# Masks of the first two weight pairs spread out of a compact block by shuffles, loads on two queues, and the first group's products cut into four batches

## The chip, the cores and the metric

The kernel runs on one core of one Trainium2 chip. The metric is the device time of one execution in microseconds (us); the kernel before takes 66.61 us (median of 3 runs, 66.33 to 66.75). Engines are named as in the profile: PE (TensorE, with its weight loads PEld), DVE (VectorE), ACT (ScalarE), POOL (GpSimd), and SP, whose queue issues most DMAs.

## The reference

```python
# B, N, T, O, G = 32, 256, 256, 256, 8; everything is f32
masked_w = weight * mask[None, :, :]              # (G, O, T)
w_bot = einsum('bg,got->bot', y, masked_w)        # y is cond_8, (B, G)
x = x + einsum('bnt,bot->bno', x, w_bot) + bias   # x is (B, N, T)
```

## The kernel before

The work has two stages. The **small stage** makes the 32 matrices `w_raw[b]` = w_bot[b] + identity (the identity carries the residual). The **large stage** multiplies the 32 batches of x by them, in 8 groups of 4 batches (`NB`), each group in two halves of the outputs, h = 0 and 1.

*Small stage.* The 256 output rows are made in 8 **units** of 32 rows (`UNITS`), two to a **pair** j. PE makes a unit u in `weigh_unit(u)` with 16 products of weight blocks with `y` (`weigh`; 32 matmul instructions in the trace, since f32 takes two passes), in four row groups of the array side by side. A unit has two sides, each a slot of 1024 columns in PSUM (`slots` 0 to 3): on the **diagonal** side PE first lays the identity down (`identity`, two bf16 matmuls), and the mask must already be in the weights, so some engine multiplies these weights by the mask before, in two halves (`masked_by_dve`, `masked_by_pool`). On the **other** side the mask is applied when the unit leaves PSUM. ACT copies the diagonal side to `w_raw` (`raw_by_act`; for unit 1 the sides are swapped), DVE multiplies the other side by its mask into `w_raw` (`raw_by_dve`). The ACT count is n+1 when unit n has left, for n of 2 or more, and so is DVE's. The first two units are made together, `weigh_first_pair`: all products of the other sides, then all of the diagonal sides. A unit may start when the slots that it writes have been emptied:

```python
            if u < SIDES:
                return slots[:, 2 * u + side, :]
            if u < EARLY:
                return slots[:, ((0, 3), (1, 2))[u % 2][side], :]

            return slots[:, ((0, 1), (3, 2))[u % 2][side], :]
```

with `EARLY = 6`. The diagonal side is 1 for even units and 0 for odd ones, so that the diagonal sides of units 2 to 7 are in slots 3, 1, 3, 1, 1, 3.

*Loads.* The data of the small stage lie in one HBM tensor `first` in the order of `ORDER`. A "masked" load of 512 KB has the diagonal weights of a pair and, beside them, their masks (each mask row 8 times, once for each g); it lands in `x_ring`, which later holds x, and the masked weights are written from there to `weights`. An "other" load (256 KB) has the weights of the other sides. All these loads are issued by SP one after the other; ACT issues the small inputs (`smalls`: y, bias and the masks of the first two other sides). DVE masks pairs 0 and 3, POOL pairs 1 and 2 and, in four pieces behind these (`raw_masked`), the side of unit 1 that ACT copied unmasked.

*Large stage.* Group 0 is multiplied in plain f32 straight from `w_raw` (`multiply_first`; a batch of one half is 2 products, 4 matmul instructions in the trace). Of its half 0, batches 0 and 1 stand on PE between units 5 and 6, in a slot of their own (`early`), the other two behind unit 7, and then half 1. Groups 1 to 7 are multiplied as three products of rounded high and low parts: for each group ACT makes `x_hi` and `w_hi`, DVE `x_lo` and `w_lo`, and PE runs 48 matmuls (`multiply_group`, 336 in all). Group 1's `w_hi` and `w_lo` are made in three pieces (`high_piece`, `low_piece`). The orders on all engines are written out by hand.

## Time and profile before

| | |
|---|---|
| median of 3 runs | 66.61 us |
| span of the profiled execution | 65.5 us |
| the profiled execution's own time | not given apart from the span; the median lies 1.1 us above the span |
| PE matmul busy | 58.8 us, 90% |
| DVE, ACT busy | 48.1 and 47.9 us, 73% each |
| POOL busy | 7.0 us, 11% |
| read and written in HBM | 11.73 and 8.39 MB |

Groups of instructions are named by line, engine, operation and tiles (out<-in). "Idle before <-X" is the time in which the engine did nothing just before, and what ended it. A queue's row such as SPq is the issue of a DMA, and its landing is given apart.

### The profile page before, as it was taken

The numbers are of one execution on the slowest core, as the hardware profiler recorded it, in microseconds if no ns is written. First come the engines' busy times: TensorE is split into PE (matmuls) and PEld (weight loads), VectorE is DVE, ScalarE is ACT, GpSimd is POOL, SyncE is SP. The second block draws the span as 40 slices with busy tenths as digits, with TensorE's granted clock in tenths as the row PEclk, the third lists the DMA queues.
The fourth block names the chain that finished last, engine by engine and source line by source line (L and its number), as shares of the span: only waits on it lengthen the run. The fifth ranks groups of instructions, "written<-read, shape, count | busy, mean of one in ns | idle before, by whom it ended". The sixth has DMA issues, their size and how long they took to land.

```text
span 65.5 us, 1501 instructions
## 1 busy us (share of the span) xinstructions
PE 58.8 (90%) x645; PEld 54.3 (83%) x645; DVE 48.1 (73%) x36; ACT 47.9 (73%) x40; POOL 7.0 (11%) x17
## 2 busy tenths in 40 slices
PE   2997188999999999999999999999999999999910
PEld 1266087977888899999999999999999999999900
DVE  2109809999957989999999999989999992250200
ACT  2506609799889999999999799999869986005520
POOL 5500299900000000000000000000000000000000
PEclk9999999999999999999999999999999999999999
DMA  0999999999998157954999999999999229918393
GB/s 0 260 373 306 352 412 422 407 434 428 420 410 340 60 85 255 408 215 198 245 285 225 400 451 420 403 441 423 398 413 425 93 100 408 398 63 325 158 372 116
DMA packets 5334, 20.21 MB, mean 309 GB/s; under 512 B 592, under 2 KB 1104, under 8 KB 4432
## 3 DMA queue, kind: packets, MB, share of 16 engines
q1 hardware_dynamic: 5040, 19.89, 79.6%
q10 hardware_dynamic: 288, 0.23, 1.1%
q8 instruction: 5, 0.08, 0.5%
q14 instruction: 1, 0.01, 0.1%
HBM read 11.73 MB, written 8.39 MB: 307 GB/s over the span
## 4 chain that ended last, share of the span: by engine, by line
PE 79%; DMA 9%; ACT 4%; SPq 2%; issue 1%
PE slots L433 20%; PE slots L431 20%; PE slots L432 20%; PE slots L451 11%; DMA weights<-in_first 9%; PE slots L332 6%; ACT w_raw L534 3%; PE slots L326 2%; ACT weights L563 1%; SPq L230 1%; SPq L222 1%; SPq L229 1%
## 5 line engine op out<-in xcount | busy, mean ns | idle before, releaser
L431 PE MATMUL slots<-x_hi,w_hi 128*128 128x256 f32 x112 | 31.4, 280 | 0.0
L432 PE MATMUL slots<-x_lo,w_hi 128*128 128x256 f32 x112 | 31.2, 279 | 0.0
L433 PE MATMUL slots<-x_hi,w_lo 128*128 128x256 f32 x112 | 31.2, 279 | 0.0
L431 PEld LDWEIGHTS slots<-x_hi,w_hi 128*128 128x128 f32 x112 | 21.1, 188 | 0.0
L432 PEld LDWEIGHTS slots<-x_lo,w_hi 128*128 128x128 f32 x112 | 21.1, 188 | 0.0
L433 PEld LDWEIGHTS slots<-x_hi,w_lo 128*128 128x128 f32 x112 | 21.1, 188 | 0.0
L589 DVE TENSOR_TENSOR x_lo<-x_ring,x_hi 128x2048 fp32r<-128x2048 f32 (+1 forms) x8 | 16.1, 2022 | 0.5 <-ACT x_hi L491 0.5
L491 ACT CAST x_hi<-x_ring 128x2048 fp32r<-128x2048 f32 (+1 forms) x8 | 13.5, 1694 | 1.3 <-DMA x_ring<-in_x 1.3
L511 ACT ACTIVATE weights<-slots,smalls 128x1024 f32<-128x1024 f32 x10 | 10.8, 1112 | 4.7 <-PE slots L433 4.7
L598 DVE TENSOR_TENSOR w_lo<-w_raw,w_hi 128x2048 fp32r<-128x2048 f32 x6 | 13.7, 2288 | 0.2 <-ACT w_hi L499 0.2
L499 ACT CAST w_hi<-w_raw 128x2048 fp32r<-128x2048 f32 x6 | 11.5, 1909 | 0.0
L332 PE MATMUL slots<-smalls,weights 32*128 32x128 f32 x256 | 9.3, 279 | 2.0 <-DMA weights<-in_first 1.6
L332 PEld LDWEIGHTS slots<-smalls,weights 32*128 32x128 f32 x256 | 8.2, 186 | 3.0 <-DVE w_raw L631 1.9
L534 ACT COPY w_raw<-slots 128x1024 f32<-128x1024 f32 x7 | 7.0, 1014 | 3.8 <-PE slots L332 3.7
L635 DVE TENSOR_TENSOR w_raw<-slots,masks_off 128x1024 f32<-128x1024 f32 x6 | 7.1, 1220 | 2.0 <-PE slots L332 1.8
L451 PE MATMUL slots<-x_ring,w_raw 128*128 128x256 f32 x32 | 7.4, 386 | 0.2
L451 PEld LDWEIGHTS slots<-x_ring,w_raw 128*128 128x128 f32 x32 | 5.9, 190 | 1.3 <-ACT w_raw L534 0.5
L615 DVE TENSOR_SCALAR weights<-slots,smalls 128x1024 f32<-128x1024 f32 x4 | 5.1, 1282 | 2.4 <-PE slots L433 2.4
L581 DVE TENSOR_TENSOR weights<-x_ring 128x256 f32<-128x256 f32 x4 | 1.5, 420 | 3.1 <-DMA x_ring<-in_first 3.1
L306 POOL TENSOR_TENSOR weights<-x_ring 128x256 f32<-128x256 f32 x4 | 2.8, 727 | 5.2 <-ACT w_raw L534 5.0
L440 PE MATMUL slots<-zeros 128*128 128x512 bf16 x5 | 2.3, 626 | 1.2 <-DVE zeros L571 1.2
L605 DVE TENSOR_TENSOR w_lo<-w_raw,w_hi 128x512 fp32r<-128x512 f32 (+1 forms) x3 | 2.5, 866 | 1.2 <-ACT w_hi L502 1.2
(25 smaller groups left out, 19.3 us busy)
## 6 DMA issues: line engine op xcount, KB each, us to landing
out<-weights SPq DMA_DIRECT2D x15, 512.0 KB, 4.7
x_ring<-in_x SPq DMA_DIRECT2D x7, 1024.0 KB, 9.6
x_ring<-in_first SPq DMA_DIRECT2D x6, 512.0 KB, 7.2
weights<-in_first SPq DMA_DIRECT2D x4, 256.0 KB, 6.6
out<-weights SPq DMA_DIRECT2D x1, 256.0 KB, 2.4
out<-weights SPq DMA_DIRECT2D x1, 128.0 KB, 2.3
out<-weights ACTq DMA_DIRECT2D x1, 128.0 KB, 2.1
smalls<-in_small ACTq DMA_DIRECT2D x1, 97.0 KB, 3.1
```

The source lines that it names most:

```text
L332: return nc.tensor.matmul(bank(u, i)[:, q * B * RT:(q + 1) * B * RT], weights_of(u, i // PER)[rows, q * P:(q + 1) * P], y[rows], start=not ...
L431: nc.tensor.matmul(dst, wh, xh, start=(k == 0), stop=False)
L432: nc.tensor.matmul(dst, wh, xl, start=False, stop=False)
L433: last = nc.tensor.matmul(dst, wl, xh, start=False, stop=(k == KC - 1))
L451: last = nc.tensor.matmul(dst[:, (b - lo) * N:(b - lo + 1) * N], w_raw[:, b, k * O + h * P:k * O + (h + 1) * P], x_ring[:, 0, first_x(k, b ...
L491: nc.scalar.copy(part_x(x_hi[:, g % RS], lo, hi), part_x(x_ring[:, g % XS], lo, hi)).then_inc(x_hi_ready, 1)
L499: nc.scalar.copy(part(w_hi, g), raw_part(g)).then_inc(w_hi_ready, 1)
L511: nc.scalar.activation(result(g, h), product(g, h), ACT.Identity, bias=bias(h)).then_inc(done, 1)
L534: nc.scalar.copy(raw_slot(u, True), made(u, True)).then_inc(raw_by_act, 1)
L589: nc.vector.tensor_tensor(part_x(x_lo[:, g % RS], lo, hi), part_x(x_ring[:, g % XS], lo, hi), part_x(x_hi[:, g % RS], lo, hi).bitcast(F32) ...
L598: nc.vector.tensor_tensor(part(w_lo, g), raw_part(g), part(w_hi, g).bitcast(F32), ALU.subtract).then_inc(w_lo_ready, 1)
L635: nc.vector.tensor_tensor(raw_slot(u, False), made(u, False), mask_off_of(u).unsqueeze(2).broadcast_to([P, PER * QU, B, RT]), ALU.mult).th ...
```

## The change

- **Masks.** The diagonal masks of pairs 0 and 1 no longer come eightfold: a compact block of 128x256 values (128 KB) is appended to `smalls`, and DVE spreads it with four `stream_shuffle` instructions of 128x256, each of which copies one row of every eight to all eight, into a quarter of the last place of `x_ring` (`mask_half`). Masks of pairs 2 and 3 still come eightfold, as 256 KB loads to the same place.
- **Loads.** The diagonal weights go straight to `weights`. From pair 1 on, diagonal and other weights of a pair are one load of 512 KB (`pair`). ACT's queue issues, behind `smalls` (97 KB before, 225 KB now), the diagonal weights of pair 0 (256 KB) and the masks of the other sides (96 KB). In all 384 KB less are read.
- **Masking.** POOL masks all four pairs in place, and `mask_raw` of unit 1 is done in one piece behind pair 1 and three behind pair 3. DVE masks none.
- **Order on PE.** `EARLY` is 4: behind each of units 4 to 7 stands one batch of group 0's half 0, in slot 1. Units 5 to 7 start with two products of the other side ahead of the identity. `unit_slot` gives units 5 to 7 the slots (3, 2), (0, 3), (3, 2).
- ACT and DVE make the first two pieces of group 1's weights one unit later or interleaved with the last units, and ACT empties group 0's half 0 in one instruction of 1024 columns, not in two of 512.

The core of the diff:

```diff
-EARLY = 6
+EARLY = 4
 WARM = 5
 
-ORDER = (("other", 0), ("masked", 0), ("masked", 1), ("other", 1), ("off", 0), ("masked", 2), ("other", 2), ("x", 0),
-         ("masked", 3), ("other", 3), ("x", 1))
-COLUMNS = {"masked": SLOT, "other": BANK, "off": (UNITS - SIDES) * SPAN, "x": WIDE // 2}
+ORDER = (("other", 0), ("masked", 0), ("pair", 1), ("off", 0), ("pair", 2), ("mask", 2), ("x", 0),
+         ("pair", 3), ("mask", 3), ("x", 1))
+COLUMNS = {"masked": BANK, "other": BANK, "pair": SLOT, "mask": BANK, "off": (UNITS - SIDES) * SPAN, "x": WIDE // 2}
...
-            if u < EARLY:
+            if u <= EARLY:
                 return slots[:, ((0, 3), (1, 2))[u % 2][side], :]
 
-            return slots[:, ((0, 1), (3, 2))[u % 2][side], :]
-
-
-        early = slots[:, 3, 0:BANK]
+            return slots[:, ((0, 3), (3, 2))[u % 2][side], :]
...
-                sp.dma_start(staged(j), in_order("masked", j)).then_inc(masked_loaded[j], 16)
-                sp.dma_start(blocks[:, 2 * j + 1, :], in_order("other", j)).then_inc(others_loaded[j], 16)
+                sp.dma_start(weights[:, j, :], in_order("pair", j)).then_inc(pair_loaded[j - 1], 16)
+                if j >= SPREAD:
+                    sp.dma_start(mask_rows[:, j * BANK:(j + 1) * BANK], in_order("mask", j)).then_inc(mask_loaded[j - SPREAD], 16)
...
                 return sp.dma_start(x_ring[:, 0, i * SLOT:(i + 1) * SLOT], in_order("x", i))
 
-            sp.dma_start(blocks[:, 1, :], in_order("other", 0)).then_inc(others_loaded[0], 16)
-            sp.dma_start(staged(0), in_order("masked", 0)).then_inc(masked_loaded[0], 16)
+            sp.dma_start(blocks[:, 1, :], in_order("other", 0)).then_inc(first_others_loaded, 16)
             load_pair(1)
-            sp.dma_start(masks_off[:].rearrange("p u m r -> p (u m r)"), in_order("off", 0)).then_inc(masks_off_loaded, 16)
             load_pair(2)
             load_half(0).then_inc(half_x_loaded, 16)
             load_pair(3)
             load_half(1).then_inc(x_loaded[0], 16)
             load_group(1)
-
-
-            sp.wait_ge(masked_by_dve, 2)
-            sp.wait_ge(masked_by_pool, 2)
-            load_group(XS - 2)
-
-            sp.wait_ge(masked_by_pool, 2 * (PAIRS - 2))
-            sp.wait_ge(masked_by_dve, 4)
+            load_group(2)
+
+            sp.wait_ge(masked_by_pool, 2 * PAIRS)
             load_group(XS - 1)
 
             for g in range(GROUPS - 1):
...
-            behind_pair = (None, (0,), (1, 2, 3))
-            for j in range(1, PAIRS - 1):
-
-                pool.wait_ge(masked_loaded[j], 16)
+            def mask_pair(j):
+
+                pool.wait_ge(first_masked_loaded if j == 0 else pair_loaded[j - 1], 16)
+                if j >= SPREAD:
+                    pool.wait_ge(mask_loaded[j - SPREAD], 16)
                 for i in range(2):
-                    nc.gpsimd.tensor_tensor(blocks[:, 2 * j, half_of(i)], staged(j)[:, 0:BANK][:, half_of(i)],
-                                            staged(j)[:, BANK:SLOT][:, half_of(i)], ALU.mult).then_inc(masked_by_pool, 1)
-
-
-                if j == 1:
-                    pool.wait_ge(smalls_loaded, 16)
-                    pool.wait_ge(raw_by_act, 1)
-                for i in behind_pair[j]:
-                    some = raw_columns(1, False)[:, i * MB:(i + 1) * MB, :]
-                    nc.gpsimd.tensor_tensor(some, some, smalls[:, AT_MASKS + SPAN:AT_MASKS + 2 * SPAN].unsqueeze(1).broadcast_to(
-                        [P, MB, SPAN]), ALU.mult).then_inc(raw_masked, 1)
+                    if j < SPREAD:
+                        pool.wait_ge(mask_spread, 2 * j + i + 1)
+                    nc.gpsimd.tensor_tensor(blocks[:, 2 * j, half_of(i)], blocks[:, 2 * j, half_of(i)],
+                                            mask_half(2 * j + i), ALU.mult).then_inc(masked_by_pool, 1)
+
+            def mask_raw(i):
+
+                some = raw_columns(1, False)[:, i * MB:(i + 1) * MB, :]
+                nc.gpsimd.tensor_tensor(some, some, smalls[:, AT_MASKS + SPAN:AT_MASKS + 2 * SPAN].unsqueeze(1).broadcast_to(
+                    [P, MB, SPAN]), ALU.mult).then_inc(raw_masked, 1)
+
+            mask_pair(0)
+            mask_pair(1)
+
+            pool.wait_ge(smalls_loaded, 16)
+            pool.wait_ge(raw_by_act, 1)
+            mask_raw(0)
+            mask_pair(2)
+            mask_pair(3)
+            for i in range(1, B // MB):
+                mask_raw(i)
 
         @block.tensor
         def _(pe):
...
-                if u < EARLY:
-
-                    pe.wait_ge(raw_by_act, u - 1)
-                elif u == EARLY:
-
-                    pe.wait_ge(raw_by_act, u)
-                else:
-
-                    pe.wait_ge(early_by_act, 1)
+                def others_first():
+
+                    pe.wait_ge(raw_by_dve, u - 1)
+                    if u % 2 == 0:
+
+                        pe.wait_ge(pair_loaded[u // 2 - 1], 16)
+                    weigh(u, off, 0)
+                    weigh(u, off + 1, 0)
+
+                if u > EARLY:
+                    others_first()
+
+                pe.wait_ge(raw_by_act, u if u > EARLY else u - 1)
                 identity(u, on)
                 identity(u, on + 1)
-
-                pe.wait_ge(raw_by_dve, u - 1)
-                if u % 2 == 0:
-
-                    pe.wait_ge(others_loaded[u // 2], 16)
-                weigh(u, off, 0)
-                weigh(u, off + 1, 0)
+                if u <= EARLY:
+                    others_first()
                 for q in range(QU):
-                    if u == EARLY and q % 2 == 0:
-
-                        pe.wait_ge(masked_by_dve, 3 + q // 2)
-                    elif u % 2 == 0 and q % 2 == 0:
-
-                        pe.wait_ge(masked_by_pool, u - 1 + q // 2)
+                    if u % 2 == 0 and q % 2 == 0:
+
+                        pe.wait_ge(masked_by_pool, u + 1 + q // 2)
...
             weigh_first_pair()
-            for u in range(SIDES, EARLY):
+            for u in range(SIDES, UNITS):
                 weigh_unit(u)
-
-
-            pe.wait_ge(raw_by_act, EARLY - 1)
-            pe.wait_ge(raw_by_dve, UNITS // HO)
-            pe.wait_ge(raw_masked, 1)
-            pe.wait_ge(half_x_loaded, 16)
-            multiply_first(early, 0, 0, NB // 2).then_inc(early_ready, 1)
-
-            for u in range(EARLY, UNITS):
-                weigh_unit(u)
-
-            pe.wait_ge(raw_by_act, UNITS - 1)
-            pe.wait_ge(x_loaded[0], 16)
-            multiply_first(product(0, 0)[:, BANK:SLOT], 0, NB // 2, NB).then_inc(products_ready, 1)
+                if u >= EARLY:
+                    b = u - EARLY
+                    if b == 0:
+
+                        pe.wait_ge(raw_by_act, UNITS // HO)
+                        pe.wait_ge(raw_by_dve, UNITS // HO)
+                        pe.wait_ge(raw_masked, 1)
+                        pe.wait_ge(half_x_loaded, 16)
+                    if b == NB // 2:
+                        pe.wait_ge(x_loaded[0], 16)
+                    last = multiply_first(product(0, 0)[:, b * N:(b + 1) * N], 0, b, b + 1)
+            last.then_inc(products_ready, 1)
             pe.wait_ge(raw_by_act, UNITS)
             pe.wait_ge(raw_by_dve, UNITS)
             multiply_first(product(0, 1), 1, 0, NB).then_inc(products_ready, 1)
...
             act.dma_start(smalls[:], small).then_inc(smalls_loaded, 16)
+            act.dma_start(blocks[:, 0, :], in_order("masked", 0)).then_inc(first_masked_loaded, 16)
+            act.dma_start(masks_off[:].rearrange("p u m r -> p (u m r)"), in_order("off", 0)).then_inc(masks_off_loaded, 16)
...
-                if u == EARLY:
+                if u == EARLY + 1:
 
                     act.wait_ge(raw_by_act, UNITS // HO)
                     act.wait_ge(raw_by_dve, UNITS // HO)
                     act.wait_ge(raw_masked, 1)
-                    high_piece(0)
-                    high_piece(1)
-
-                    act.wait_ge(smalls_loaded, 16)
-                    act.wait_ge(early_ready, 1)
-                    nc.scalar.activation(result(0, 0)[:, 0:BANK], early, ACT.Identity, bias=bias(0)).then_inc(early_by_act, 1)
+                if u in (EARLY + 1, EARLY + 2):
+                    high_piece(u - EARLY - 1)
 
                 act.wait_ge(diagonal_ready, u + 1)
                 nc.scalar.copy(raw_slot(u, True), made(u, True)).then_inc(raw_by_act, 1)
...
-            mask_pair(0)
+            dve.wait_ge(smalls_loaded, 16)
+            compact = smalls[:, AT_COMPACT:AT_COMPACT + COMPACT]
+            for c in range(CHUNKS):
+                nc.vector.stream_shuffle(mask_half(c), compact, [G * (i // G) + c for i in range(ROWS)]).then_inc(mask_spread, 1)
```

On PE, from behind unit 5 on, before: L451 is a product of group 0, L326 the identity, L332 a product of a unit. The rows are two batches, unit 6, and the identity of unit 7.

```order
L451 MATMUL slots<-x_ring,w_raw 128x256 [waits raw_masked,half_x_loaded,raw_by_dve,raw_by_act]
L451 MATMUL slots<-x_ring,w_raw 128x256 x3
L326 MATMUL slots<-one_of,one_at 128x512 [waits raw_by_act]
L326 MATMUL slots<-one_of,one_at 128x512
L332 MATMUL slots<-smalls,weights 128x128 [waits others_loaded3,raw_by_dve]
L332 MATMUL slots<-smalls,weights 128x128
L332 MATMUL slots<-smalls,weights 128x128 [waits masked_by_dve]
L332 MATMUL slots<-smalls,weights 128x128 x7
L332 MATMUL slots<-smalls,weights 128x128 [waits masked_by_dve]
L332 MATMUL slots<-smalls,weights 128x128 x5
L326 MATMUL slots<-one_of,one_at 128x512 [waits early_by_act]
L326 MATMUL slots<-one_of,one_at 128x512
```

PE now, from behind unit 4 on: L453 is a product of group 0, L332 the identity, L338 a product of a unit. The rows are a batch, unit 5, a batch, and the start of unit 6.

```order
L453 MATMUL slots<-x_ring,w_raw 128x256 [waits raw_masked,half_x_loaded,raw_by_dve,raw_by_act]
L453 MATMUL slots<-x_ring,w_raw 128x256
L338 MATMUL slots<-smalls,weights 128x128 [waits raw_by_dve]
L338 MATMUL slots<-smalls,weights 128x128
L332 MATMUL slots<-one_of,one_at 128x512 [waits raw_by_act]
L332 MATMUL slots<-one_of,one_at 128x512
L338 MATMUL slots<-smalls,weights 128x128 x14
L453 MATMUL slots<-x_ring,w_raw 128x256 x2
L338 MATMUL slots<-smalls,weights 128x128 [waits pair_loaded3,raw_by_dve]
L338 MATMUL slots<-smalls,weights 128x128
L332 MATMUL slots<-one_of,one_at 128x512 [waits raw_by_act]
L332 MATMUL slots<-one_of,one_at 128x512
```

Before, two batches stood in one block behind unit 5; now one batch stands behind each unit, and every identity from unit 5 on waits for ACT's copy of the unit just ahead.

The DMAs that SP issues for the small stage before, in order:

```order
L229 DMA weights<-in_first 128x512
L230 DMA x_ring<-in_first 128x1024
L222 DMA x_ring<-in_first 128x1024
L223 DMA weights<-in_first 128x512
L232 DMA masks_off<-in_first 128x192
L222 DMA x_ring<-in_first 128x1024
L223 DMA weights<-in_first 128x512
L227 DMA x_ring<-in_first 128x1024
L222 DMA x_ring<-in_first 128x1024
L223 DMA weights<-in_first 128x512
L227 DMA x_ring<-in_first 128x1024
```

SP's issues now, up to the second half of group 0's x (the row with x2 is pairs 1 and 2), and behind them the start of ACT's order:

```order
L233 DMA weights<-in_first 128x512
L225 DMA weights<-in_first 128x1024 x2
L227 DMA x_ring<-in_first 128x512
L231 DMA x_ring<-in_first 128x1024
L225 DMA weights<-in_first 128x1024
L227 DMA x_ring<-in_first 128x512
L231 DMA x_ring<-in_first 128x1024
```

```order
L483 DMA smalls<-in_small 128x450
L484 DMA weights<-in_first 128x512
L485 DMA masks_off<-in_first 128x192
L518 ACT_TABLE_LOAD
L518 COPY w_raw<-slots 128x8x32x4 [waits others_ready]
L532 COPY w_raw<-slots 128x8x32x4 [waits diagonal_ready] x4
```

The diagonal weights of pair 0 moved from SP's second place to ACT's queue behind `smalls`, and pair 1, with both its sides, to SP's second place.

On POOL, the masking before:

```order
L306 TENSOR_TENSOR weights<-x_ring 128x256 [waits masked_loaded1]
L306 TENSOR_TENSOR weights<-x_ring 128x256
L315 TENSOR_TENSOR w_raw<-w_raw,smalls 128x8x32 [waits raw_by_act,smalls_loaded]
L306 TENSOR_TENSOR weights<-x_ring 128x256 [waits masked_loaded2]
L306 TENSOR_TENSOR weights<-x_ring 128x256
L315 TENSOR_TENSOR w_raw<-w_raw,smalls 128x8x32 x3
```

and now:

```order
L304 TENSOR_TENSOR weights<-weights,x_ring 128x256 [waits mask_spread,first_masked_loaded]
L304 TENSOR_TENSOR weights<-weights,x_ring 128x256 [waits mask_spread]
L304 TENSOR_TENSOR weights<-weights,x_ring 128x256 [waits mask_spread,pair_loaded1]
L304 TENSOR_TENSOR weights<-weights,x_ring 128x256 [waits mask_spread]
L310 TENSOR_TENSOR w_raw<-w_raw,smalls 128x8x32 [waits raw_by_act,smalls_loaded]
L304 TENSOR_TENSOR weights<-weights,x_ring 128x256 [waits mask_loaded2,pair_loaded2]
L304 TENSOR_TENSOR weights<-weights,x_ring 128x256
L304 TENSOR_TENSOR weights<-weights,x_ring 128x256 [waits mask_loaded3,pair_loaded3]
L304 TENSOR_TENSOR weights<-weights,x_ring 128x256
L310 TENSOR_TENSOR w_raw<-w_raw,smalls 128x8x32 x3
```

Four more instructions stand here, two of them in front of everything else.

## Rows read from the trace of the kernel before

**Rows 1.** Page, chain that ended last: shares of the span by engine.
```profile
PE 79%; DMA 9%; ACT 4%; SPq 2%; issue 1%
```

**Rows 2.** Windows: length, busy time by engine, granted clock, DMA share, GB/s.
```profile
core 0: us, PE busy (x) PEld busy (x) DVE busy (x) ACT busy (x) POOL busy (x), PEclk, DMA share, GB/s
4.00:8.00 4.00, 2.43 (x70) 1.85 (x66) 3.02 (x4) 2.02 (x2) 0.29 (x1) 1.00 0.96 331
8.00:12.00 4.00, 3.35 (x98) 3.20 (x102) 2.21 (x3) 1.97 (x2) 3.80 (x7) 1.00 1.03 414
23.30:62.40 39.10, 39.10 (x336) 38.89 (x334) 32.28 (x18) 32.15 (x24) 0.00 (x0) 1.00 0.81 305
```

**Rows 3.** Loads: issue (start us, us), then KB and us to landing.
```profile
weights<-in_first SPq DMA_DIRECT2D x1, 256.0 KB, 2.9
smalls<-in_small ACTq DMA_DIRECT2D x1, 97.0 KB, 3.1
1.17 0.43 SPq L230 DMA_DIRECT2D x_ring<-in_first  x1
x_ring<-in_first SPq DMA_DIRECT2D x1, 512.0 KB, 3.8
1.65 0.42 SPq L222 DMA_DIRECT2D x_ring<-in_first  x1
x_ring<-in_first SPq DMA_DIRECT2D x1, 512.0 KB, 6.0
```

**Rows 4.** Timeline of PE: start us, us, instructions [idle before, releaser].
```profile
5.46 1.17 PE L332 MATMUL slots<-smalls,weights 32*128 32x128 f32 x32 [0.41 <-DVE weights L581]
8.43 1.34 PE L332 MATMUL slots<-smalls,weights 32*128 32x128 f32 x30 [1.59 <-DMA weights<-in_first]
...
11.00 0.39 PE L326 MATMUL slots<-one_of,one_at 32*128 32x512 bf16 x2 [0.22 <-ACT w_raw L534]
12.08 0.39 PE L326 MATMUL slots<-one_of,one_at 32*128 32x512 bf16 x2
...
13.42 1.99 PE L451 MATMUL slots<-x_ring,w_raw 128*128 128x256 f32 x8
15.35 0.39 PE L326 MATMUL slots<-one_of,one_at 32*128 32x512 bf16 x2
...
17.75 5.45 PE L451 MATMUL slots<-x_ring,w_raw 128*128 128x256 f32 x24
22.84 0.47 PE L431 MATMUL slots<-x_hi,w_hi 128*128 128x256 f32 x1
```

**Rows 5.** Timeline of ACT: units 2, then 4 and 5, then group 0.
```profile
9.93 1.02 ACT L534 COPY w_raw<-slots 128x1024 f32<-128x1024 f32 x1 [2.24 <-PE slots L332]
12.36 2.14 ACT L534 COPY w_raw<-slots 128x1024 f32<-128x1024 f32 x2 [0.46 <-PE slots L332]
25.48 0.68 ACT L545 ACTIVATE weights<-slots,smalls 128x512 f32<-128x512 f32 x1
```

**Rows 6.** Timeline of POOL: the masks of pair 1.
```profile
7.71 1.41 POOL L306 TENSOR_TENSOR weights<-x_ring 128x256 f32<-128x256 f32 x2 [5.05 <-ACT w_raw L534]
```

**Rows 7.** Timeline of DVE: masks of pair 0, units 6 and 7, x_lo of group 2.
```profile
4.99 0.76 DVE L581 TENSOR_TENSOR weights<-x_ring 128x256 f32<-128x256 f32 x2 [3.11 <-DMA x_ring<-in_first]
...
16.56 2.36 DVE L635 TENSOR_TENSOR w_raw<-slots,masks_off 128x1024 f32<-128x1024 f32 x2
...
26.00 2.29 DVE L589 TENSOR_TENSOR x_lo<-x_ring,x_hi 128x2048 fp32r<-128x2048 f32 x1
```

**Rows 8.** Windows, behind the last matmul.
```profile
62.50:65.30 2.80, 0.00 (x0) 0.00 (x0) 0.00 (x0) 0.41 (x1) 0.00 (x0) 1.00 0.66 244
65.38:65.46 0.08, 0.00 (x0) 0.00 (x0) 0.00 (x0) 0.00 (x0) 0.00 (x0) 0.57 0.00 0
```

More of the change, by code:

```diff
@@ L675, with diagonal_of @@
     w_rows, m_rows = rows_of(weight), rows_of(np.broadcast_to(mask, (G, O, T)))
-    diagonal = [np.stack((a[2 * j + 1][0], a[2 * j][0])).reshape(P, BANK) for j in range(PAIRS) for a in (w_rows, m_rows)]
+    def diagonal_of(a, j):
+        return np.stack((a[2 * j + 1][0], a[2 * j][0])).reshape(-1, BANK)
+    mask_in = np.concatenate([diagonal_of(m_rows, j) for j in range(SPREAD)], axis=1)
+    mask_in = np.concatenate([mask_in[r, r % CHUNKS * COMPACT:(r % CHUNKS + 1) * COMPACT] for r in range(P)]).reshape(P, COMPACT)
     loads = {}
     for j in range(PAIRS):
-        loads["masked", j] = np.concatenate(diagonal[2 * j:2 * j + 2], axis=1)
-        loads["other", j] = np.stack((w_rows[2 * j][1], w_rows[2 * j + 1][1]))
+        other = np.stack((w_rows[2 * j][1], w_rows[2 * j + 1][1])).reshape(P, BANK)
+        if j == 0:
+            loads["masked", 0], loads["other", 0] = diagonal_of(w_rows, 0), other
+        else:
+            loads["mask", j] = diagonal_of(m_rows, j)
+            loads["pair", j] = np.concatenate([diagonal_of(w_rows, j), other], axis=1)
     for i in range(2):
```

48 lines of the change are left out of this document (21 added, 27 removed).

## The prediction

> **What bounds the kernel now.** The page comes first: PE holds 79% of the chain that ended last, DMA 9% and ACT 4% [rows 1]. The windows say where the small shares lie: from 23.30 to 62.40 PE is busy without a gap, 336 matmuls in 39.10 us [rows 2], so a group of 48 takes 5.59 us, and nothing in this change touches a matmul of it. What the change can win or lose lies ahead of the first of them, at 22.84 [rows 4], and the matter is when this one starts. The timeline of PE shows the waits there: 1.59 us until 8.43 for the loads of pair 1, 0.22 until 11.00 for ACT's copy of unit 2 [rows 4], and small ones behind. I call 11.00, the start of unit 4's identity, the **hand-over**. From there to group 1 it is 11.84 us.
>
> **Loads.** I write L for the time at which the diagonal weights of pair 0 have landed. Before, they landed with their masks at 1.17 + 3.8 = 4.97, with 865 KB in all issued up to them (256 + 97 + 512). Pair 1's masked load landed at 1.65 + 6.0 = 7.65, at 1377 KB [rows 3]. Between the two stand 512 KB in 2.68 us, 191 KB per us, though the engines move 414 GB/s from 8 to 12 us and 331 from 4 to 8 [rows 2]: a load has landed when its slowest share has.
>
> Now the weights of pair 0 stand behind 225 KB of smalls on ACT's queue, beside SP's queue. Which queue goes ahead is seen in one place: the 256 KB on SP's queue and the 97 KB on ACT's were issued together and landed after 2.9 and 3.1 us [rows 3], so neither waited for all of the other. If the queues take turns row by row, the 256 rows ahead on ACT's queue (128 of smalls, 128 of weights) go beside 256 rows of SP's, 128 of 2 KB and 128 of 4 KB: 225 + 256 + 256 + 512 = 1249 KB, which on the line through the two landings is 4.97 + 384/191 = 6.98. The nearest row of a landing is that at 1377 KB, 7.65. SP's queue ran alone while smalls were still starting, so that more than 1249 KB may be ahead: I take **L = 7.3**, bounds 5.9 (1249 KB with no laggard: 384 KB at 414 GB/s behind 4.97) and 7.65. The Trainium skill ("DMA: Bandwidth & Descriptors", Issuing engines are not separate DMA queues) says that DMAs of different engines run on the same 16 DMA engines and interleave, and that a second issuing engine saves only issue time. The two landings agree. By it, the second queue brings pair 0 nothing, and the sum keeps L = 7.3; without it L could be that of a queue served first, which is a rival below.
>
> **First pair to hand-over.** POOL now masks pairs 0 and 1, four multiplications. Two took 1.41 us together and began 0.06 us behind the landing, at 7.71 [rows 6]; DVE's two took 0.76 [rows 7]. The four end at L + 0.06 + 2.82 = L + 2.88. From the end of pair 1's masks (7.71 + 1.41 = 9.12) to the hand-over it took 11.00 − 9.12 = 1.88 [rows 4, 6]: the rest of unit 2 on PE, ACT's copy of 1.02 from 9.93 [rows 5], and the identity. So the hand-over is at L + 4.76 = 12.06, **1.06 later** than before. PE does not bind there: the first pair's 32 matmuls take 1.17 us [rows 4] and follow the masks half by half. The shuffles are not in the trace. The nearest rows are DVE's multiplications of the same 128x256 values, 0.38 each [rows 7]; even at double that, the four would end at about 4.3 + 3.0 = 7.3, beside the load of the weights, and only the first two are wanted by L + 0.8. I take 0. If the weights landed by 5, that cover would be gone, and the first shuffle would cost up to 0.8. The 384 KB that are no longer read make pairs 2 and 3 and x land earlier; the waits of PE before were not for these, so this is 0. A gain is not excluded where pair 1 lands earlier, but POOL comes to it only at L + 1.5.
>
> **Hand-over to group 1.** Units 4, 5, 6 and 7 all put their diagonal side in slot 3 now, so each identity waits for ACT's copy of the unit ahead. A turn of this ring: identity to copy 12.36 − 11.00 = 1.36 [rows 4, 5], copy 1.01 (half of the 2.14 of two, less the wait between them; the single one is 1.02), and copy to identity 11.00 − 10.95 = 0.05, together 2.42. PE has less to do in a turn: a unit is 12.08 − 11.00 = 1.08, a batch is four of the 24 instructions that ran from 17.75 to 22.84, 0.85 [rows 4]; 1.93 in all, so 0.5 us of each turn PE stands. Three turns take unit 7's identity to hand-over + 7.26. Then half 1 of group 0 waits for both sides of unit 7: DVE's multiplication began 16.56 − 15.35 = 1.21 behind an identity and takes 1.2 (two take 2.36) [rows 4, 7], with 0.05 to PE 2.47. Half 1 is 16 instructions, 3.39. Sum 7.26 + 2.47 + 3.39 = 13.12, against 11.84: **1.28 later**. The wait for DVE's masks of pair 3, ahead of unit 6, and that for `early` are inside the 11.84 and go; late instead is the ring. Bounds: 1.93 a turn if the ring did not bind (4 × 1.93 + 3.39 = 11.1, −0.7), and 2.6 if ACT's first piece of group 1's weights, which now stands between the copies of units 4 and 5, were to touch it; PE's 1.36 hides it.
>
> **Groups 1 to 7.** Before, `x_lo` of group 2 was ready at 28.29 [rows 7], when PE came for it at 22.84 + 5.59 = 28.43, 0.14 to spare. ACT and DVE work off the same list behind unit 7, so that counts from the end of DVE's unit 7, 16.56 + 2.36 = 18.92: ready 9.37 later. PE now comes 0.05 + 3.39 + 5.59 = 9.03 behind it, since only half 1 stands there and not 12 of group 0's 16 products: a wait of 0.34. ACT's finishing of group 0's half 0 goes over 1024 columns instead of 512 (0.68 [rows 5]), which may push `x_hi` of group 4 by some tenths. I take **0.4** for both, bounds 0 and 0.6. Load 3 of x waits for all of POOL's masks, at about L + 7, and is needed far behind.
>
> **The sum.** 1.06 + 1.28 + 0.4 = 2.74 on the span of 65.5, 68.2; the median of 66.61 lies 1.1 above the span, so **69.35**. With L from 6.98 to 7.65 and the groups' bounds it is 68.7 to 69.9.
>
> **Rivals.**
> *The clock falls.* PE's longest wait before, 1.59, left the granted clock at 1.00. Now PE has nothing from some 5.4 (first pair's other sides, a little later than before) until L + 0.8 = 8.1, 2.7 us. Behind the last matmul the clock was 1.00 up to 65.30 and fell inside 65.38 to 65.46 (0.57 is a mean of both levels), 3.0 us behind PE's end [rows 8]; so 2.7 lies near. At 1.2 GHz the units' 1.1 us become 2.2 for some us: the first pair's second half +0.5, unit 2 +0.5, unit 3 +0.5, together 1.5, time 70.85. For: the gap. Against: it is shorter than that at the end, and work stands around it. The Trainium skill ("TensorE: Matmul & The Clock Gate", Part 1) says that the full clock is withdrawn when the array has been idle; by that this rival holds if the idle stretch is long enough.
> *ACT's queue goes first.* Pair 0 then lands with about as much ahead as before, near 5, and pair 1 is last, with all 1249 to 1345 KB ahead, 7.0 to 7.5. POOL masks it at once: hand-over 7.25 + 0.06 + 1.41 + 1.88 = 10.6, 0.4 earlier, sum +1.3, **67.9**.
> *No laggards.* This is the one on the other side. The slow shares between 5 and 7.65 need not come again, and then pairs 0 and 1 both land at about 5.9. In the better order the hand-over is at 5.9 + 3.35 = 9.25, −1.75; the ring still costs 1.28, the groups 0 to 0.4: −0.5 to −0.1, **66.3**. It decides from a hand-over of 9.3 on; to be faster by over 1% it would have to be 8.7, or the ring not bind. Against: there are 2.7 us between two landings 512 KB apart.
> *The change doesn't do what it says.* If the shuffles took over 1 us each, the masks would be late and not the weights; that would look like the forecast, with DVE as releaser, and cost more.
>
> **Numbers.** About 1% of the time, 0.67 us, is what a measurement of this kernel can tell from no change. Forecast 0.55; clock 0.15; ACT's queue first 0.15; no laggards 0.12; the rest 0.03. No laggards gives half of "same" and some of "faster", the second rival a little of "same": faster 0.05, same 0.11, slower 0.84. The range runs from the lower end of the second rival, 67.3, to the clock's price, 70.8; below lie some 0.13, above 0.05.
>
> **What would show it.** The landing of pair 0's diagonal weights between 7.0 and 7.65, and POOL's first mask right behind it; the identity of unit 4 near 12.1; identities of units 5, 6, 7 spaced by 2.42, with ACT's copy as releaser and about 0.5 idle on PE each time; group 1's first matmul near 25.2; a wait of some 0.3 on DVE's `x_lo` at group 2; 39.1 us of matmuls as before. A landing by 6, or units spaced by less than 2.1, would make the forecast wrong; so would a granted clock under 1 between 8 and 14.

## The result: 70.69 us, slower by the ratio 1.0553 (1.0434 to 1.0671)

| | before | after |
|---|---|---|
| median (runs) | 66.47 us (66.24 to 66.75, 4) | 70.69 us (69.66 to 70.79, 4) |
| a profiled execution: time, span | 66.33, 64.5 us (e7, below) | 70.79, 68.7 us |
| read in HBM | 11.73 MB | 11.34 MB |

The ratio rests on the runs within 1.5% of the fastest of each kernel, for the changed one 70.60 and 69.66; the medians stand at 1.0635. Spans of its four runs: 68.7, 68.7, 68.5 and 67.5.

The timeline of PE after the change; the rows answer to [rows 4] (start, length, instructions, idle before and its releaser; L338 is a product of a unit, L332 the identity, L453 a product of group 0, L433 a group's product):

```profile
4.34 1.17 PE L338 MATMUL slots<-smalls,weights 32*128 32x128 f32 x32 [0.30 <-DMA smalls<-in_small]
7.38 1.99 PE L338 MATMUL slots<-smalls,weights 32*128 32x128 f32 x32 [1.86 <-POOL weights L304]
9.12 0.64 PE L332 MATMUL slots<-one_of,one_at 32*128 32x512 bf16 x2
9.15 2.02 PE L338 MATMUL slots<-smalls,weights 32*128 32x128 f32 x30
...
12.40 0.39 PE L332 MATMUL slots<-one_of,one_at 32*128 32x512 bf16 x2 [0.21 <-ACT w_raw L532]
...
14.82 0.39 PE L332 MATMUL slots<-one_of,one_at 32*128 32x512 bf16 x2
...
17.22 0.39 PE L332 MATMUL slots<-one_of,one_at 32*128 32x512 bf16 x2
...
19.62 0.39 PE L332 MATMUL slots<-one_of,one_at 32*128 32x512 bf16 x2
...
22.13 3.69 PE L453 MATMUL slots<-x_ring,w_raw 128*128 128x256 f32 x16 [0.17 <-DVE w_raw L625]
25.57 0.39 PE L433 MATMUL slots<-x_hi,w_hi 128*128 128x256 f32 x1
```

The first row's 32 instructions take 1.17 us, the second's 1.99: the granted clock reads 1.00 from 7.0 to 7.5 and 0.55 from 7.5 to 8.0, so it fell just behind the start of the second row. The hand-over (unit 4's identity) is at 12.40, the four identities from there on stand 2.40 to 2.42 apart, and group 1 starts at 25.57. The windows (length, busy time of PE, PEld, DVE, ACT and POOL, granted clock, DMA share, GB/s) answer to [rows 2] and show the clock and the groups:

```profile
8.00:10.00 2.00, 2.00 (x44) 2.00 (x41) 0.56 (x1) 0.62 (x1) 2.00 (x5) 0.50 1.03 416
10.00:12.00 2.00, 2.00 (x59) 1.99 (x54) 1.47 (x2) 1.06 (x2) 1.48 (x3) 0.76 1.03 399
12.00:14.00 2.00, 1.79 (x44) 1.44 (x37) 1.85 (x3) 1.54 (x3) 2.00 (x4) 1.00 1.06 426
25.57:65.45 39.88, 39.88 (x337) 39.68 (x336) 33.02 (x18) 33.34 (x24) 0.00 (x0) 1.00 0.78 296
```

The DMA issues of the start (KB, us to landing), answering to [rows 3]:

```profile
weights<-in_first SPq DMA_DIRECT2D x1, 512.0 KB, 4.9
weights<-in_first SPq DMA_DIRECT2D x1, 256.0 KB, 3.4
weights<-in_first ACTq DMA_DIRECT2D x1, 256.0 KB, 5.4
smalls<-in_small ACTq DMA_DIRECT2D x1, 225.0 KB, 3.6
```

and POOL's and DVE's timelines, answering to [rows 6] and [rows 7]:

```profile
6.60 2.78 POOL L304 TENSOR_TENSOR weights<-weights,x_ring 128x256 f32<-128x256 f32 x4 [3.96 <-DMA weights<-in_first]
```

```profile
4.33 0.01 DVE L577 LOAD_MASK_SELECT x_ring<-smalls  x1 [2.46 <-DMA smalls<-in_small]
4.33 0.44 DVE L577 STREAM_SHUFFLE x_ring<-smalls 128x256 f32<-128x256 f32 x1
...
29.07 2.28 DVE L582 TENSOR_TENSOR x_lo<-x_ring,x_hi 128x2048 fp32r<-128x2048 f32 x1
```

Pair 0's diagonal weights, issued by ACT at 1.18, landed 5.4 later, at L = 6.53 by their semaphore; POOL starts on them at 6.60. The four shuffles lie well ahead, 0.34 apart (the next at 4.67, 5.02 and 5.36).

**A second look at before.** The profile of before that the prediction was read from turned out to be a late one. In 53 timed runs of before beside the experiments, 32 spans lie between 64.2 and 64.8 and the other 21 between 65.1 and 66.4; that profile's is 65.5. The run e7, the same kernel again, has a span of 64.5. PE and POOL there, beside [rows 4] and [rows 6]:

```profile
9.65 0.39 PE L326 MATMUL slots<-one_of,one_at 32*128 32x512 bf16 x2
...
21.91 0.47 PE L431 MATMUL slots<-x_hi,w_hi 128*128 128x256 f32 x1
```

```profile
6.34 1.42 POOL L306 TENSOR_TENSOR weights<-x_ring 128x256 f32<-128x256 f32 x2 [3.69 <-DMA x_ring<-in_first]
```

```profile
21.91:61.19 39.28, 39.28 (x338) 39.26 (x336) 32.66 (x18) 32.62 (x24) 0.00 (x0) 1.00 0.80 301
```

Pair 1's masked load is there at 6.3, not 7.65, and the hand-over at 9.65, not 11.00, the same 1.35 earlier. The windows of the groups run from the start of the first of their matmuls to the start of the last. Set against this typical execution (66.33 us), the changed one (70.79) loses 4.46 in four places: hand-over 12.40 − 9.65 = 2.75; from there to group 1, 13.17 − 12.26 = 0.91; the groups' matmuls 39.88 − 39.28 = 0.60; outside the span 2.09 − 1.83 = 0.26 (the rest, −0.06, lies behind the last matmul).

### The profile page after: what moved, and what is told of

The parts are those of the page before. It is cut to its first block, busy times and chain, and to the rows that moved or that the text cites. A ratio compares the mean times of both kernels' runs of the same rounds, so it can differ in the third digit from the quotient of the medians.

```text
span 68.7 us, 1506 instructions
## 1 busy us (share of the span) xinstructions
PE 62.0 (90%) x645; PEld 56.5 (82%) x645; DVE 48.4 (70%) x40; ACT 47.7 (69%) x39; POOL 9.7 (14%) x21
## 3 DMA queue, kind: packets, MB, share of 16 engines
HBM read 11.34 MB, written 8.39 MB: 287 GB/s over the span
## 4 chain that ended last, share of the span: by engine, by line
PE 81%; DMA 5%; issue 3%; DVE 2%; ACT 2%; POOL 1%; POOLq 0%
PE slots L433 20%; PE slots L435 19%; PE slots L434 19%; PE slots L338 12%; PE slots L453 10%; DMA smalls<-in_small 5%; DVE w_raw L625 2%; ACT w_raw L532 1%; PE slots L332 1%; POOL weights L304 1%; ACT weights L560 1%; DVE x_ring L577 1%; POOLq L303 0%
## 5 line engine op out<-in xcount | busy, mean ns | idle before, releaser
L433 PE MATMUL slots<-x_hi,w_hi 128*128 128x256 f32 x112 | 31.7, 283 | 0.0
L433 PEld LDWEIGHTS slots<-x_hi,w_hi 128*128 128x128 f32 x112 | 21.0, 188 | 0.3
L513 ACT ACTIVATE weights<-slots,smalls 128x1024 f32<-128x1024 f32 x11 | 12.0, 1121 | 5.1 <-PE slots L435 5.1
L338 PEld LDWEIGHTS slots<-smalls,weights 32*128 32x128 f32 x256 | 10.3, 219 | 3.9 <-POOL weights L304 2.1
L338 PE MATMUL slots<-smalls,weights 32*128 32x128 f32 x256 | 11.4, 310 | 2.2 <-POOL weights L304 1.9
L453 PE MATMUL slots<-x_ring,w_raw 128*128 128x256 f32 x32 | 8.2, 393 | 0.2 <-DVE w_raw L625 0.2
L453 PEld LDWEIGHTS slots<-x_ring,w_raw 128*128 128x128 f32 x32 | 5.7, 189 | 1.6 <-ACT w_raw L532 0.5
L304 POOL TENSOR_TENSOR weights<-weights,x_ring 128x256 f32<-128x256 f32 x8 | 5.6, 725 | 4.5 <-DMA weights<-in_first 4.0
L332 PE MATMUL slots<-one_of,one_at 32*128 32x512 bf16 x16 | 3.2, 475 | 0.2 <-ACT w_raw L532 0.2
```

The costliest lines, as they stand in the source:

```text
L338: return nc.tensor.matmul(bank(u, i)[:, q * B * RT:(q + 1) * B * RT], weights_of(u, i // PER)[rows, q * P:(q + 1) * P], y[rows], start=not ...
L433: nc.tensor.matmul(dst, wh, xh, start=(k == 0), stop=False)
L453: last = nc.tensor.matmul(dst[:, (b - lo) * N:(b - lo + 1) * N], w_raw[:, b, k * O + h * P:k * O + (h + 1) * P], x_ring[:, 0, first_x(k, b ...
L513: nc.scalar.activation(result(g, h), product(g, h), ACT.Identity, bias=bias(h)).then_inc(done, 1)
```

## The experiments

"Ratio" is against the runs of before on the same chip. Hand-over, group 1's start and span are of the profiled execution. An interval that lies wholly above 1 shows a loss, whatever its size; where two intervals overlap, the medians alone don't tell the two kernels apart, and the argument rests on the traces.

| run | median (range), us | ratio (95%) | hand-over | group 1 | span |
|---|---|---|---|---|---|
| e1 filled | 69.97 (69.58–70.63) | 1.0504 (1.0342–1.0666) | 11.17 | 24.39 | 67.6 |
| e2 one queue | 68.84 (68.16–69.15) | 1.0343 (1.0165–1.0521) | 10.06 | 23.39 | 66.6 |
| e3 old order | 68.76 (67.86–69.37) | 1.0264 (1.0037–1.0491) | 11.31 | 23.21 | 65.8 |
| e4 ring alone | 68.47 (67.89–69.06) | 1.0268 (1.0117–1.0420) | 10.62 | 23.79 | 66.8 |
| e5 both | 68.03 (67.24–68.18) | 1.0240 (1.0191–1.0289) | 11.45 | 23.29 | 65.9 |
| e6 both, filled | 67.29 (66.95–67.73) | 1.0142 (1.0097–1.0187) | 11.07 | 23.08 | 65.7 |
| e7 before again | 66.33 (one run) | | 9.65 | 21.91 | 64.5 |
| e8 after again | 70.82 (one run) | | 12.55 | 25.73 | 68.7 |
| e9 split | 67.46 (67.14–68.23) | 1.0101 (1.0032–1.0171) | 10.75 | 22.77 | 65.7 |
| e10 more smalls | 66.72 (66.38–67.83) | 1.0046 (1.0009–1.0082) | 10.03 | 21.97 | 64.6 |
| e11 before filled | 66.91 (66.15–67.61) | 1.0036 (0.9993–1.0080) | 10.58 | 22.42 | 65.1 |
| e12 off on ACT | 66.35 (66.26–66.79) | 1.0000 (0.9965–1.0036) | 10.00 | 21.84 | 64.5 |

**e1, the clock.** The changed kernel, with eight products of zeros added to the slots while PE waits for the first masks (they change no value).

```diff
+FILL = 8
...
+                for f in range(FILL):
+                    last_on = bank(f // 2 % 2, on[f // 2 % 2] + f % 2)
+                    nc.tensor.matmul(last_on, zeros[:, 0:P], zeros[:], start=False, stop=False)
```

> The changed kernel with eight bf16 matmuls of zeros added to the first pair's diagonal banks (they add nothing) between its two halves of products, where PE stands for about 1.9 us. Theory: the granted clock fell to 1.2 GHz for 3.4 us because PE stood there, and that cost 1.1 us up to the hand-over (12.40 measured, 9.38 + 1.88 = 11.26 without it). Then the clock stays at 1.00, the hand-over is near 11.3 and the time near 69.5. Rival, the clock fell but the masks set the pace anyway: hand-over stays near 12.4, time 70.7.

The windows from 8 to 12, with the granted clock at 1.00, and PE's hand-over:

```profile
8.00:12.00 4.00, 4.00 (x112) 3.54 (x114) 3.15 (x3) 2.69 (x3) 3.53 (x6) 1.00 1.04 409
```

```profile
7.29 1.41 PE L339 MATMUL slots<-smalls,weights 32*128 32x128 f32 x32
...
11.17 0.39 PE L333 MATMUL slots<-one_of,one_at 32*128 32x512 bf16 x2
```

With the wait filled the clock stays, and from the first masked product to the hand-over it takes 11.17 − 7.29 = 3.88 instead of 12.40 − 7.38 = 5.02: the fall costs 1.14 in the trace. The medians differ by 0.72 and the intervals overlap, since e1's own spans scatter (67.6, 68.6, 67.6, 68.3). All four have a mean clock of 1.00, so the clock is not all that makes a run of this kernel long.

**e2, the queue.** Pair 0's diagonal weights second on SP's queue, as before.

```diff
+            sp.dma_start(blocks[:, 0, :], in_order("masked", 0)).then_inc(first_masked_loaded, 16)
...
-            act.dma_start(blocks[:, 0, :], in_order("masked", 0)).then_inc(first_masked_loaded, 16)
```

> The changed kernel with one DMA moved: the diagonal weights of pair 0 are issued second on SP's queue, as before, not on ACT's behind the small inputs. Theory: the place on ACT's queue delayed their landing (6.53 measured); now it is near 5.0, POOL's fourth mask ends by 7.9, the hand-over is near 9.8, PE never stands long enough for the clock to fall, and the time is near 68.0. Rival, the masks of POOL or the bandwidth set the pace and not the queue: hand-over above 11, time over 69.3.

POOL and PE:

```profile
5.12 2.79 POOL L305 TENSOR_TENSOR weights<-weights,x_ring 128x256 f32<-128x256 f32 x4 [2.47 <-DMA weights<-in_first]
```

```profile
4.26 3.41 PE L339 MATMUL slots<-smalls,weights 32*128 32x128 f32 x64 [0.22 <-DMA smalls<-in_small]
```

L is 5.04 instead of 6.53, POOL starts 1.48 earlier, PE has no gap, and the hand-over comes 2.34 earlier. The place on the queue behind the small inputs cost 1.5 us of landing, and through it the clock. The first pair's 64 instructions now run through in 3.41 us, where 32 at the full clock take 1.17, so the clock rose late; the hand-over is L + 5.02.

**e3, the order.** The changed kernel's loads and masks, with the order of before on PE, ACT and DVE, and its slots (`EARLY = 6`). The diff shows the two lines that decide it; the waits and pieces of before go with them.

```diff
-EARLY = 4
+EARLY = 6
...
-            return slots[:, ((0, 3), (3, 2))[u % 2][side], :]
+            return slots[:, ((0, 1), (3, 2))[u % 2][side], :]
```

> The changed kernel with the old order of the last units: EARLY = 6, the old slots, the two batches of group 0 in one block behind unit 5, the other two behind unit 7; loads and masks as changed. Theory: the ring over slot 3 cost 1.3 us from the hand-over to group 1 and 0.4 to 0.6 in the groups; hand-over still 12.4, group 1 at 12.4 + 11.84 = 24.2, time near 69.0. Rival, PE would have waited elsewhere anyway: group 1 at 25.3 or later, time 70.5.

PE up to the hand-over:

```profile
4.33 1.76 PE L345 MATMUL slots<-smalls,weights 32*128 32x128 f32 x32 [0.28 <-DMA smalls<-in_small]
7.42 1.41 PE L345 MATMUL slots<-smalls,weights 32*128 32x128 f32 x32 [1.33 <-POOL weights L311]
...
11.31 0.39 PE L339 MATMUL slots<-one_of,one_at 32*128 32x512 bf16 x2
```

From the hand-over to group 1 it took 23.21 − 11.31 = 11.90, close to the 11.84 of [rows 4], against 13.17. Up to the hand-over PE's order is that of the changed kernel, its wait there was 1.33, and in this execution the clock did not fall. The wait was shorter only because the 32 instructions ahead of it took 1.76 and not 1.17, that is, because the clock rose later: the second row starts at 7.42 here and at 7.38 there. So the length of the wait and the time of the rise changed together, and this run does not say which of the two spared the clock. Two more of its runs had a mean clock of 0.970 and 0.992 and spans of 66.9 and 67.3, 1.1 and 1.5 more. Its L + 4.74 (L = 6.57) is the length of the first stretch without a fall.

**e4, the order alone.** The kernel before with the changed order, slots and pieces; the diff shows its first lines.

```diff
-EARLY = 6
+EARLY = 4
...
-            return slots[:, ((0, 1), (3, 2))[u % 2][side], :]
+            return slots[:, ((0, 3), (3, 2))[u % 2][side], :]
```

> The kernel before with only the new order of the last units: EARLY = 4, the new slots, one batch behind each of units 4 to 7; loads and masks as before. Theory: hand-over stays at 11.0, identities of units 4 to 7 are 2.4 apart, group 1 starts 13.1 later, at 24.1 instead of 22.8, and the groups lose 0.4 more: time 66.5 + 1.7 = 68.2. Rival, the order is neutral and all of the loss came from the loads and masks: time 66.5.

A turn of the ring in it:

```profile
13.04 0.39 PE L321 MATMUL slots<-one_of,one_at 32*128 32x512 bf16 x2
13.13 1.19 PE L327 MATMUL slots<-smalls,weights 32*128 32x128 f32 x30
14.25 1.13 PE L445 MATMUL slots<-x_ring,w_raw 128*128 128x256 f32 x4
15.31 0.38 PE L327 MATMUL slots<-smalls,weights 32*128 32x128 f32 x2
15.44 0.39 PE L321 MATMUL slots<-one_of,one_at 32*128 32x512 bf16 x2
```

The turns take 2.40 and group 1 starts at hand-over + 13.17, the same to the hundredth as in the changed kernel. The order alone makes the kernel slower, by 1.2 to 4.2% in the interval, and needs no change of loads for it.

**e5, both undone.** e2 and e3 together: of the change only the masks by shuffle and the masking on POOL stay.

> The changed kernel with both suspected costs undone: diagonal weights of pair 0 second on SP's queue, and the old order and slots of the last units. What is left of the change is the compact masks, the shuffles, the masks on POOL and 384 KB less to read. Theory: hand-over near 9.8 as in the run with one queue (10.06), group 1 11.84 later at 21.7, against 22.8 to 23 before: 1 us less of span, of which 0.2 are given back outside the span; time about 0.7 us under the kernel before. Rival, the groups' own chain on DVE eats the lead: no difference.

```profile
4.49 4.00 PE L346 MATMUL slots<-smalls,weights 32*128 32x128 f32 x66 [0.45 <-DMA smalls<-in_small]
8.08 0.64 PE L340 MATMUL slots<-one_of,one_at 32*128 32x512 bf16 x2
8.28 1.72 PE L346 MATMUL slots<-smalls,weights 32*128 32x128 f32 x26
```

Here my account fell: the hand-over was awaited at 9.8 and came at 11.45, though POOL began at 5.30. PE's first 66 instructions take 61 ns each, the pace of the 62 ns that the changed kernel has at a granted clock of 0.50, and keep it up to 10 us. Waits for loads were gone, and the slow pace of a late rise took their place.

**e6, both undone and filled.** Two zero products ahead of the first pair and two between its halves, on top of e5.

> The run before this one with four matmuls of zeros more (they add nothing): two behind the first identities, where PE waits for the small inputs, and two between the first pair's halves. The clock rose at 7.14 in the profile of the run with one queue and the first pair's products ran at 1.2 GHz until then. Theory: when PE stands less in the first 6 us, the rise comes at 4 to 5 more often and the time is 0.3 to 0.7 us lower in the mean and less spread. Rival, the rise depends on something else: no difference, or 0.2 slower.

The median is 0.74 less than e5's, and the intervals of the ratios just don't meet. The identity of unit 3 comes at 9.80, as e5's (9.77), but that of unit 4 at 11.07: its first 32 instructions took 2.09 us, the next 32, from 7.53 on, 1.17, so that the clock rose at about 7. It confirms the clock's part in e5, and leaves 1.4%. How much of this is still the clock's is open: the first 32 instructions ran at half pace here too, and the profile lists no wait of PE from 7.53 to the hand-over.

**e7 and e8, both kernels again.** No edit.

> The kernel before, unchanged, for a second profile. Theory: the late landings of its profile (7.63 for the masks of pair 1, where most shares were there by 6.2) and the hand-over at 11.00 are not typical, since most of its timed runs have spans of 64.3 to 65.5 with the 65.5 of the profile at the upper end; a second profile shows a landing by 7.0 and a hand-over between 10.2 and 10.8. Rival, the laggards are the rule: landing 7.6 again.

> The changed kernel, unchanged, for a second profile. Theory: whether the clock falls behind 7.5 depends on when PE's wait comes, since the run with the old order did the same up to unit 4 with a granted clock of 1.00 and a hand-over at 11.31. Without a fall the hand-over is 11.3 and the span 67.5 to 67.7; with one it is 12.4 and 68.7. The landing of pair 0's diagonal weights is at 6.4 to 6.6 either way. Rival, the landing wanders: below 6 or above 7.

e7 is told above. e8 repeats the changed kernel's profile, with the fall of the clock behind a wait of 1.74 (window 8 to 12):

```profile
4.34 1.32 PE L338 MATMUL slots<-smalls,weights 32*128 32x128 f32 x32 [0.29 <-DMA smalls<-in_small]
7.39 1.93 PE L338 MATMUL slots<-smalls,weights 32*128 32x128 f32 x32 [1.74 <-POOL weights L304]
8.00:12.00 4.00, 4.00 (x82) 3.92 (x80) 2.06 (x2) 1.52 (x2) 3.52 (x7) 0.57 1.03 406
```

**e9, the small inputs split.** e5, with the 97 KB of before in one DMA and the compact masks (128 KB) in the next.

```diff
-            act.dma_start(smalls[:], small).then_inc(smalls_loaded, 16)
+            act.dma_start(smalls[:, 0:AT_COMPACT], small[:, 0:AT_COMPACT]).then_inc(smalls_loaded, 16)
+            act.dma_start(smalls[:, AT_COMPACT:SMALL], small[:, AT_COMPACT:SMALL]).then_inc(compact_loaded, 16)
```

> The kernel with both costs undone, and the small inputs in two DMAs on ACT's queue: y, bias and the first masks (97 KB) as before, then the compact masks (128 KB), for which only the shuffles wait. Theory: with both costs undone the kernel was still 1.5 us slower than before because the small inputs came at 4.45 instead of 3.82, so PE stood early, and the granted clock rose only at 10.1 in its profile; the first pair ran at 1.2 GHz. Now the small inputs are there by 3.9, the clock rises at 4 to 6, the hand-over is at 9.7 to 10.0 and the time near 66.7, of which 0.25 are outside the span. Rival, the masks on POOL or the DVE's shuffles are what is left: hand-over still above 10.8 and time above 67.5.

```profile
4.09 1.29 PE L347 MATMUL slots<-smalls,weights 32*128 32x128 f32 x32
6.45 1.41 PE L347 MATMUL slots<-smalls,weights 32*128 32x128 f32 x32 [1.07 <-POOL weights L313]
```

```profile
5.67 1.41 POOL L313 TENSOR_TENSOR weights<-weights,x_ring 128x256 f32<-128x256 f32 x2 [3.02 <-DVE x_ring L598]
7.45 1.41 POOL L313 TENSOR_TENSOR weights<-weights,x_ring 128x256 f32<-128x256 f32 x2 [0.37 <-DMA weights<-in_first]
```

PE starts 0.4 earlier than in e5 and at the full clock's pace, the hand-over is 0.70 earlier. Now the shuffles (from 5.09) are what POOL waits for (5.67), behind a compact block that landed 3.9 after its issue. In this execution POOL also waits 0.37 for pair 1's load, which landed at 7.4. This is the best form that I found with shuffled masks, and by its ratio it is still 1.0% slower than before (0.3 to 1.7%).

**e10, the size of the small inputs.** The kernel before, with 128 KB that nobody reads added to `smalls`.

> The kernel before with 128 KB more in the small inputs' DMA, which nothing reads; all else as before. Theory: the small inputs land near 4.3 instead of 3.8, PE stands 0.5 us longer before the first pair, the clock rises later, and the time is 0.6 to 1.4 us above the kernel before. The time outside the span stays at 1.8 if the 0.25 more of the changed kernels are not a matter of this DMA's size. Rival, half a microsecond later is all: 0.3 to 0.5 us slower, with the clock's rise where it was.

This is a miss: the loss is 0.5%, 0.3 us, and not 0.6 to 1.4; the expectation's own rival had it. The small inputs landed 0.3 later than in before, and that is nearly all it cost.

**e11, before filled.** Two zero products ahead of its first pair.

> The kernel before with two matmuls of zeros (they add nothing), one behind the first identities and one between the first pair's sides. Theory: before, PE stands little in the first 6 us and the clock is up by about 5; two fillers bring at most 0.2 us, and the slower of its timed runs (span 65.2 to 65.7) come less often if they are runs with a late rise, and as often if they are runs with late landings. Rival, they delay the first pair: 0.2 slower.

There is no gain, and spans of 65.1 to 65.8 kept coming, in 8 of 12 runs; the profiled one (65.1) had pair 1's masks at 7.21, and its first pair at the full clock's pace. Both profiles of such runs, this one and that of before, show a late landing and not a late clock; the others have no profile.

**e12, a load on ACT's queue.** The kernel before, `masks_off` issued by ACT.

```diff
-            sp.dma_start(masks_off[:].rearrange("p u m r -> p (u m r)"), in_order("off", 0)).then_inc(masks_off_loaded, 16)
...
+            act.dma_start(masks_off[:].rearrange("p u m r -> p (u m r)"), in_order("off", 0)).then_inc(masks_off_loaded, 16)
```

> The kernel before with one DMA moved: the masks of the other sides (96 KB) are issued by ACT behind the small inputs, not by SP. It asks where the 0.25 us outside the span come from: the kernels with one DMA on ACT's queue at the start have a time 1.8 us above their span, those with two or three 2.0 to 2.2. Theory: each further DMA on ACT's queue at the start adds some tenths there; the time stands 2.0 above the span here, and 0.1 to 0.3 above the kernel before. Rival, it belongs to the shuffles on DVE: 1.8 here, and no difference in time.

The time is that of before, and 1.76 to 1.85 lie outside the span as before: a second DMA on ACT's queue is not what the changed kernel pays there. The theory fell.

## Why the prediction was right in sign and too low

The direction, and the two stretches blamed for it, held: the forecast was 69.35 (67.3 to 70.8), the median is 70.69. The path did not hold in full. By the prediction's own signs a granted clock under 1 between 8 and 14 us would make the forecast wrong, and it read 0.50 there; the measured time lies beside the rival "the clock falls" (70.85), and near the upper end of the range. That it lies so near is in part luck, since that rival kept an L that was too late and a fall that was too dear.

Told as differences, 2.74 was forecast and the changed execution loses 4.46 against e7. Of the 1.72 between them 1.69 lie at the hand-over, where 1.06 was forecast and 2.75 measured: before's own hand-over is 9.65 and not 11.00 (1.35), the clock's fall adds 1.11, and the earlier L takes off 0.77. The ring takes off 0.37 more, the groups add 0.20, the time outside the span 0.26, and the end takes off 0.06. By the steps of the prediction:

- **The hand-over of before.** This is the largest term that was mis-sized. 11.00 was read from one late execution, while the median of 66.61 came from typical ones, so that a delay of 1.06 was counted where its own hand-over of 12.06 is 2.4 behind a typical one.
- **L, mis-sized.** It was 6.53 and not 7.3, outside the sign of 7.0 to 7.65. The line through two landings took the 7.65 of pair 1 for a matter of the bytes ahead. e7 has the same load at 6.3 with the same bytes ahead: it was a late share of one execution. With no such share L lies between the bound of 5.9 and the forecast. That ACT's queue brings pair 0 nothing held: e2 brings it 1.5 us forward on SP's. "ACT's queue goes first" (near 5) is out.
- **L to hand-over.** It took 5.87 and not 4.76. The four POOL masks (2.78 for 2.82) and 4.76 in all were right where the clock stayed: 4.74 in e3. The rival "the clock falls", given 0.15, came on top of the forecast in both profiles of the changed kernel, for 1.1 instead of 1.5, after waits of 1.86 and 1.74, not 2.7. The price rests on e1 and e3 against the changed kernel. The step that failed is the comparison with the wait at the end of [rows 8], read as evidence that a shorter one is safe. The Trainium skill ("TensorE: Matmul & The Clock Gate", Part 1) has an idle array lose its full clock. The granted 0.50 from 8 to 10 us, behind a wait, agrees, while e3, with a wait of 1.33 in the same place, kept it. The fall was not in all runs: one of 68.7 us had a mean clock of 0.999, and what made that one long is not shown.
- **Shuffles at 0.** This was right in the changed kernel: they are over at 5.80, ahead of L. In e5 the profile names a shuffle as what POOL waited for (5.30), but the first mask needs only the first shuffle, over at 4.91, and the weights landed at 5.24. Only in e9, where the weights land at 4.87 and the shuffles start at 5.09, does POOL wait for a shuffle, 0.8 behind the landing, as the text said of that cover.
- **The ring.** This is the best term: turns of 2.40 to 2.42 for 2.42, and 13.17 to group 1 for 13.12, unit 7 and half 1 as laid out. In all five profiles with the new order it is 13.17 to 13.33. Its cost is 1.33 against the late execution of before, 1.27 against e3, which has the same loads (11.90), and 0.91 against e7, which hands over earliest (9.65) and takes 12.26. e12 and e10, also of the old order and with spans of 64.5 and 64.6, take 11.84 and 11.94; what held e7 up is not shown.
- **Groups.** They cost 0.60, the upper bound, and not 0.4. The wait for `x_lo` is there: DVE ends it at 29.07 + 2.28 = 31.35, and group 2 starts at 31.40, against 25.57 + 5.59 = 31.16, so 0.24 for 0.34. A second, similar one stands at group 4. All the kernels with the new order have 39.68 to 39.90, and e3, e5 and e6, with the old one, 39.27 and 39.28. But e9, also of the old order, has 39.71 with a wait for `x_lo` at group 2, so that the order is not all that can bring it.
- **Outside the span, and the base.** 1.1 was the median of typical runs less the span of a late one. In the 53 runs of before it is 1.75 to 1.94, so a base of 65.5 belonged to about 67.3 us, and a typical base is 64.5. That the forecast of the span, 68.2, came out only 0.5 short of 68.7 is luck: the base was too high by 1.0 and stood against a change that cost 4.2 where 2.74 was forecast. For the changed kernel 2.07 to 2.16 lie outside. All kernels with the shuffles have 1.98 to 2.24 and all without 1.75 to 1.94. Neither the size of the small inputs (e10) nor a second DMA on ACT (e12) makes it; whether the shuffles do stays open, since none was tried without the compact masks' data and POOL's work that go with them.

"No laggards" was half true, and no help: the landings of the changed kernel were regular, and the time still grew, since pair 0 landed at 6.53 and not at 5.9, and before had no laggards in its usual runs either.

What is left of the change once queue, order and most of the clock are undone (e6, e9) still costs 1.0 to 1.4%. Two masks of 0.7 each that stood on DVE now stand in front of POOL's two for pair 1. In e9 POOL ends pair 1's masks at 8.86, in e7 at 7.76, and the hand-over is later by the same 1.10; of this 0.37 is the wait for pair 1's load, and the rest is POOL's work and wait for pair 0 ahead. That shows the path in one execution against one; no run isolates it.

## What to carry to other kernels

Before building on one profile, set its span beside those of the timed runs: here the profile and the median belonged to different executions, and 1.0 us went wrong by it. A load that the first step needs goes ahead on its own queue: here, behind 225 KB on a second queue, it landed 1.5 us later than in second place on SP's. When work is moved so that every step waits for a copy of the one just ahead, add up one turn of that ring: the sum of three rows gave its price to 0.05 us.
